# A fused recurrent scan: 32-column products, half-precision expert products in blocks of 8 steps, and another order on VectorE

## The reference, cut to what matters

```
# layer 1: a GRU cell over time, then a linear layer plus one of 8 rank-16 experts
gi = x @ W_ih + b_ih;  gh = h @ W_hh + b_hh
r = sigmoid(i_r + h_r);  z = sigmoid(i_z + h_z);  n = tanh(i_n + r * h_n)
h_new = (1.0 - z) * n + z * h
base_out = einsum('bsd,od->bso', x, W_base) + b_base
expert_idx = argmax(softmax(einsum('bsd,ed->bse', x, router_W)))
h = einsum('bsd,erd->bser', x, A) * onehot(expert_idx)[..., None]
out = base_out + einsum('bser,eor->bso', h, Bw) * 2
x = x + out
# layer 2: Runge-Kutta 4, four derivatives a step, x is the drive
i_couple = tanh(q) @ coupling.T
dq = q - q ** 3 / 3.0 - p + drive + i_couple + bias
dp = EPSILON * (q + ALPHA - BETA * p)
```

## Time and profile before

| | |
|---|---|
| median of the runs | 5070.73 us (5060.59 to 5075.04) |
| profiled execution | 5060.11 us, span 5058.5 us |
| TensorE busy | 4811.2 us (95%) |
| VectorE busy | 2748.1 us (54%) |
| ScalarE busy | 1687.5 us (33%) |
| GpSimd busy | 357.5 us (7%) |
| mean granted TensorE clock | 0.781 |

### The profile page before, as it was taken

The page is one execution under the profiler, slowest core; times in us unless marked ns, Lnnn a source line. Parts: engine busy times, 40 slices in busy tenths (PEclk is TensorE's granted clock), DMA queues, the critical chain, the costliest instruction groups (busy, mean ns, idle before and its releaser), DMA issues. The chain is left out here.

```text
span 5058.5 us, 197415 instructions
## 1 busy us (share of the span) xinstructions
PE 4811.2 (95%) x83680; PEld 3821.2 (76%) x83680; DVE 2748.1 (54%) x15134; ACT 1687.5 (33%) x7030; POOL 357.5 (7%) x1123
## 2 busy tenths in 40 slices
PE   8999989699999999999998699999999999999999
PEld 3335654699999999999997588789999999444444
DVE  3110020488888888888888726575553342344421
ACT  1101111245555555555554322233322221233320
POOL 1100010011111111111111100000000000000000
PEclk7999989555555555555555599999989999899999
DMA  3202330000000000000001000023320000100000
GB/s 106 106 10 111 150 124 8 16 4 5 5 5 5 5 5 5 5 5 5 5 5 53 13 9 2 33 71 94 92 77 3 3 3 2 47 8 8 10 7 33
DMA packets 52292, 159.62 MB, mean 32 GB/s; under 512 B 13873, under 2 KB 14001, under 8 KB 46272
## 3 DMA queue, kind: packets, MB, share of 16 engines
q1 hardware_dynamic: 45408, 130.70, 7.7%
q0 software_dynamic: 3712, 12.29, 0.7%
q10 hardware_dynamic: 2304, 4.20, 0.2%
HBM read 129.63 MB, written 17.17 MB: 29 GB/s over the span
## 5 line engine op out<-in xcount | busy, mean ns | idle before, releaser
L631 PE MATMUL k_ps<-k_hx,k_wlo 128*128 128x8 f16 x16384 | 604.9, 169 | 95.5 <-ACT k_hx L723 95.0
L631 PEld LDWEIGHTS k_ps<-k_hx,k_wlo 128*128 128x128 f16 x16384 | 545.7, 105 | 135.2 <-ACT k_hx L723 111.0
L634 PE MATMUL k_ps<-k_hl,k_whi 128*128 128x16 f16 x16384 | 590.0, 174 | 2.9 <-issue 0.4
L634 PEld LDWEIGHTS k_ps<-k_hl,k_whi 128*128 128x128 f16 x16384 | 519.4, 104 | 7.4 <-issue 1.8
L631 PE MATMUL g_ps<-g_hx,g_wlo 128*128 128x8 f16 x12288 | 434.2, 168 | 47.1 <-DVE g_hx L802 41.9
L634 PE MATMUL g_ps<-g_hl,g_whi 128*128 128x16 f16 x12288 | 436.9, 174 | 4.2 <-issue 4.1
L631 PEld LDWEIGHTS g_ps<-g_hx,g_wlo 128*128 128x128 f16 x12288 | 384.9, 104 | 59.0 <-DVE g_hx L802 52.3
L634 PEld LDWEIGHTS g_ps<-g_hl,g_whi 128*128 128x128 f16 x12288 | 385.1, 104 | 4.4 <-issue 4.4
L723 ACT ACTIVATE k_hx<-k_q 128x32 f16<-128x32 f32 x768 | 176.1, 229 | 567.1 <-DVE k_q L863 564.1
L1475 DVE TENSOR_REDUCE t_NM<-t_ps 128x1 f32<-128x512 f32 x256 | 165.0, 686 | 218.3 <-PE t_ps L1341 218.3
L863 DVE TENSOR_REDUCE k_q<-k_ps 128x32 f32<-128x96 f32 x768 | 196.8, 256 | 147.6 <-PE k_ps L634 122.0
(11 more groups left out here) (340 smaller groups left out, 8994.4 us busy)
## 6 DMA issues: line engine op xcount, KB each, us to landing
GRZ<-expert_places SPq DMA_DIRECT2D x64, 512.0 KB, 4.9
wm<-in_w_dram SPq DMA_DIRECT2D x4, 2816.0 KB, 10.2
GRZ<-in_w_dram SPq DMA_DIRECT2D x4, 2816.0 KB, 9.8
m_w<-in_w2a_dram SPq DMA_DIRECT2D x8, 1280.0 KB, 12.6
GRZ<-in_ue_dram SPq DMA_DIRECT2D x8, 1024.0 KB, 7.9
GRZ<-in_x_nat_dram SPq DMA_DIRECT2D x4, 1024.0 KB, 10.3
XT<-in_xT_dram SPq DMA_DIRECT2D x1, 4096.0 KB, 26.9
expert_rows<-wm SPq DMA_DIRECT2D x1, 4096.0 KB, 17.3
```

Source lines behind the costliest of these rows:

```text
L631: T.matmul(P[:,1,j*NB:(j+1)*NB],lo[:,kc,(m0+j)*128:(m0+j+1)*128],x[:,kc,:],start=(j==0 and kc==0),stop=False,skip_group_check=True)
L634: i=T.matmul(P[:,:,j*NB:(j+1)*NB],hi[:,kc,(m0+j)*128:(m0+j+1)*128],x[:,kc,:,:],start=False,stop=kc==KC-1,skip_group_check=True)
```

## The change

Five things are done together; what is computed stays the same.

1. Each gate and evaluation product streams 32 columns: the 8-column vector is read four times over (a broadcast view), the 16-column pair twice, and the copies land in unused columns of the same PSUM bank. The number of products and of weight loads stays.
2. Layer 1's base matrix, router and first factor are also split into two half-precision parts (by GpSimd, four passes over 2592 columns at the start of the scan). Each full-precision call becomes three half-precision ones (high weights by both state parts, low weights by the state). The states are now stored as half-precision parts for a whole block (`HX`, `HL`), and the full-precision state as two rows (`HF`).
3. Blocks of TL = 8 steps (64 columns) and LEAD = 17 rather than 16 and 29. Of every 8 iterations seven hold expert work: i = 0 and 1 six router products and three base products each, i = 2 and 4 fifteen base products each, i = 3 twelve and a transpose, i = 5 and 6 two full-precision calls each of the second factor.
4. The block's result is no longer added by VectorE (L826, which waited for TensorE), but copied out of PSUM by ScalarE (`expert_out`) and added by GpSimd (`results`); the bias is added once, by GpSimd, at the start.
5. VectorE's order: the limit of q (`limit`) is taken out of `end`; the z gate's `pre` comes first in an iteration, `low_part(t,0)` ahead of G0 and Q, `diff` leaves the place ahead of evaluation 3's `end` for evaluation 0, Q1 goes from evaluation 0 to 1, `state_full` behind evaluation 0's `end`, `low(s)` behind `low_part(t,1)`, and `low_part(t,2)` ahead of `pre(s,R_)`.

```diff
-LEAD, TL = 29, 16
+LEAD, TL = 17, 8
...
-        hx=sb('g_hx',[128,KC,NB],F16); hl=sb('g_hl',[128,KC,2,NB],F16); HS=sb('g_HS',[128,2,KC,TL,NB])
+        hx0=sb('g_hx0',[128,KC,NB],F16); hl0=sb('g_hl0',[128,2,KC,NB],F16); HF=sb('g_HF',[128,2,32]); HX=sb('g_HX',[128,2,KC,TL,NB],F16); HL=sb('g_HL',[128,2,2,KC,TL,NB],F16)
...
-                    T.matmul(P[:,1,j*NB:(j+1)*NB],lo[:,kc,(m0+j)*128:(m0+j+1)*128],x[:,kc,:],start=(j==0 and kc==0),stop=False,skip_group_check=True)
+                    T.matmul(P(j),lo[:,kc,(m0+j)*128:(m0+j+1)*128],bc(x[:,kc,:].unsqueeze(1),[128,4,NB]),start=(j==0 and kc==0),stop=False,skip_group_check=True)
-                    i=T.matmul(P[:,:,j*NB:(j+1)*NB],hi[:,kc,(m0+j)*128:(m0+j+1)*128],x[:,kc,:,:],start=False,stop=kc==KC-1,skip_group_check=True)
+                    i=T.matmul(P(j),hi[:,kc,(m0+j)*128:(m0+j+1)*128],bc(x(kc).unsqueeze(1),[128,2,2,NB]),start=False,stop=kc==KC-1,skip_group_check=True)
...
-                hs=HS[:,j%2].rearrange('p d t b -> p d (t b)')
+                hx=HX[:,j%2].rearrange('p d t b -> p d (t b)'); hS=HL[:,j%2,0].rearrange('p d t b -> p d (t b)'); lS=HL[:,j%2,1].rearrange('p d t b -> p d (t b)')
+                def base(u0,u1):
+                    for u in range(u0,u1):
+                        dc,d=u//4,u%4
+                        P=pso[:,dc*TN:(dc+1)*TN]; wh=wbh[:,d,dc*128:(dc+1)*128]; wl=wbl[:,d,dc*128:(dc+1)*128]
+                        T.matmul(P,wh,hS[:,d,:],start=u==0,stop=False,skip_group_check=True)
+                        T.matmul(P,wh,lS[:,d,:],start=False,stop=False,skip_group_check=True)
+                        T.matmul(P,wl,hx[:,d,:],start=False,stop=False,skip_group_check=True)
                 if i<2:
                     if i==0:
-                        e.wait_ge(g_h,TL*(j+1))
-                        if j==0: e.wait_ge(s_lw,64)
+                        e.wait_ge(g_lo,TL*(j+1)+1)
+                        if j==0: e.wait_ge(s_sp,4)
+                        e.wait_ge(l_e,j)
                     for d in (2*i,2*i+1):
-                        x=T.matmul(psh[:,0:136],hs[:,d,:],ar[:,d,:],start=d==0,stop=d==3)
+                        T.matmul(psh[0:TN,0:136],hS[:,d,:],arh[:,d,:],start=d==0,stop=False)
+                        T.matmul(psh[0:TN,0:136],lS[:,d,:],arh[:,d,:],start=False,stop=False)
+                        x=T.matmul(psh[0:TN,0:136],hx[:,d,:],arl[:,d,:],start=False,stop=d==3)
                     if i==1: x.then_inc(l_h,1)
-                if i==2: e.wait_ge(l_x,4*j)
-                if 2<=i<10:
-                    for u in (2*(i-2),2*(i-2)+1):
-                        dc,d=u//4,u%4
-                        T.matmul(pso[:,dc*128:(dc+1)*128],wb[:,d,dc*128:(dc+1)*128],hs[:,d,:],start=u==0,stop=False,skip_group_check=True)
-                if i==4:
+                    base(i,i+1)
+                if i==2: base(2,7)
+                if i==3:
+                    base(7,11)
                     e.wait_ge(l_ht,j+1)
-                    T.transpose(pst[:,0:128],ht[:],K.ident[:]).then_inc(l_tr,1)
-                if i in (10,11):
+                    T.transpose(pst[:,0:TN],ht[:],K.ident[0:TN,0:TN]).then_inc(l_tr,1)
+                if i==4: base(11,16)
+                if i in (5,6):
                     e.wait_ge(l_hm,j+1)
-                    for dc in (2*(i-10),2*(i-10)+1):
-                        x=T.matmul(pso[:,dc*128:(dc+1)*128],bw[:,dc*128:(dc+1)*128],hm[:],start=False,stop=True,skip_group_check=True)
-                    if i==11: x.then_inc(l_o,1)
+                    for dc in (2*(i-5),2*(i-5)+1):
+                        x=T.matmul(pso[:,dc*TN:(dc+1)*TN],bw[:,dc*128:(dc+1)*128],hm[:],start=False,stop=True,skip_group_check=True)
+                    if i==6: x.then_inc(l_o,1)
...
+            def expert_out(s):
+                j,i=s//TL-1,s%TL
+                if i!=7 or j<0 or j>=NT//TL: return
+                e.wait_ge(l_o,j+1)
+                if j>0: e.wait_ge(l_x,j)
+                A.activation(ex[:].rearrange('p d t b -> p (d t b)'),pso[:,0:KC*TN],ACT.Copy,scale=US).then_inc(l_e,1)
...
+            def results(s):
+                j,i=s//TL-1,s%TL
+                if i!=7 or j<0 or j>=NT//TL: return
+                e.wait_ge(l_e,j+1)
+                x=XT[:,:,:,j*TL:(j+1)*TL].rearrange('p d b t -> p d t b')
+                G.tensor_tensor(x,ex[:],x,ALU.add).then_inc(l_x,1)
+            e.wait_ge(s_lw,64)
+            both=wm[:,0:2592]; high,low_=split[:,0:2592],split[:,2592:5184]
+            G.tensor_scalar(both,both,SW,None,ALU.mult).then_inc(s_sp,1)
+            e.wait_ge(s_sp,1)
+            G.tensor_copy(high,both).then_inc(s_sp,1)
+            e.wait_ge(s_sp,2)
+            G.tensor_tensor(both,both,high,ALU.subtract).then_inc(s_sp,1)
+            e.wait_ge(s_sp,3)
+            G.tensor_scalar(low_,both,S,None,ALU.mult).then_inc(s_sp,1)
+            for dc in range(KC): G.tensor_scalar(XT[:,dc],XT[:,dc],bb[:,dc:dc+1],None,ALU.add).then_inc(s_bx,1)
...
-                elif i==12:
-                  e.wait_ge(l_o,j+1)
-                  for dc in (2*part,2*part+1):
-                    x=XT[:,dc,:,j*TL:(j+1)*TL].rearrange('p b t -> p t b')
-                    V.scalar_tensor_tensor(x,pso[:,dc*128:(dc+1)*128].rearrange('p (t b) -> p t b',b=NB),bb[:,dc:dc+1],x,ALU.add,ALU.add).then_inc(l_x,1)
...
-                e.wait_ge(k_q,t*4+k+2)
-                if k==3:
-                    e.wait_ge(k_out,t)
-                    V.tensor_scalar(q[:,0,:],qn[:],20.0/uq[0],-20.0/uq[0],ALU.min,ALU.max).then_inc(k_q0,1)
+                if k<3: e.wait_ge(k_q,t*4+k+2)
+            def limit(t):
+                e.wait_ge(k_q,t*4+5)
+                e.wait_ge(k_out,t)
+                V.tensor_scalar(q[:,0,:],qn[:],20.0/uq[0],-20.0/uq[0],ALU.min,ALU.max).then_inc(k_q0,1)
             for t in range(NT):
                 s=t+LEAD
+                if t>0:
+                    pre(s-1,Z_)
+                    limit(t-1)
+                    arg(s-1,Z_)
+                low_part(t,0)
+                if t>0: diff(s-1)
                 e.wait_ge(k_q0,t+1)
                 n_G=ch.did(stt(G0[:],p[:],-BETA*6/h,q[:,0,:]))
                 e.wait_ge(k_u,t+1)
                 n_Q=ch.did(stt(Q[:,0,:],q[:,0,:],1/3,E0[:]))
-                if t>0: pre(s-1,Z_)
-                low_part(t,0)
-                if t>0: arg(s-1,Z_)
+                if t>0: upd(s-1)
                 cubic(t,0)
-                ch.after(max(n_G,n_Q))
-                n_Q1=ch.did(stt(Q[:,1,:],G0[:],-a*EPS*h/6,Q[:,0,:]))
+                if t>0: state_half(s-1)
                 total(t,0,Q[:,0,:],n_Q)
-                if t>0: upd(s-1); state_half(s-1); state_full(s-1)
                 end(t,0)
 
+                if t>0: state_full(s-1)
                 e.wait_ge(k_aq,t*2+2)
                 n_B=ch.did(stt(B0[:,0,:],G0[:],-a*EPS*(1-kap)*h/6,AQ[:,0,:]))
                 n_C=ch.did(stt(B0[:,1,:],G0[:],cD,AQ[:,1,:]))
+                low_part(t,1)
+                n_Q1=ch.did(stt(Q[:,1,:],G0[:],-a*EPS*h/6,Q[:,0,:]))
                 low(s)
-                low_part(t,1)
                 ch.after(n_B)
                 n_K=ch.did(V.tensor_tensor(K2[:],Q[:,0,:],B0[:,0,:],ALU.add))
                 ch.after(n_C)
...
                 ch.after(max(n_W,n_X))
                 n_X=ch.did(stt(X[:,1,:],q[:,1,:],3*(1/3+e2*kap),X[:,0,:]))
                 n_W=ch.did(stt(W[:,1,:],q[:,1,:],a*hh*(2-2*kap+2*kap*kap),W[:,0,:]))
+                low_part(t,2)
                 pre(s,R_)
-                low_part(t,2)
                 arg(s,R_)
                 cubic(t,2)
                 ch.after(max(n_W,n_X))
...
                 ch.after(n_p)
                 V.tensor_scalar(p[:],pn[:],(20.0-SHIFT)/US,(-20.0-SHIFT)/US,ALU.min,ALU.max).then_inc(k_p,1)
                 total(t,3,X[:,3,:],n_X)
-                diff(s)
                 end(t,3)
+            limit(NT-1)
```

59 lines of the change are left out of this document (34 added, 25 removed).

## The result

The changed kernel takes 4980.18 us (median of 4 runs, 4976.26 to 5004.06) against 5065.66 (4 runs, 5055.51 to 5075.04) beside it: ratio 0.9845, 95% interval 0.9822 to 0.9868. It is faster by 1.55%. Forecast were 4820 us and a range from 4770 to 4965, so the direction was right and the gain a third of what was forecast; the time lies above the range. The profiled execution took 4976.7 us, with a span of 4975.1 against 5058.5.

The account below looks back on a forecast made before the run. The prediction took a chain of dependent steps to bound the scan's iteration, 7.36 us falling to 6.52. Lead -52, main part -113, tail -85 and GpSimd's split +3 sum to -247: 4813, median 4820 us, range 4770 to 4965.

Parts of the forecast that it names:

- VectorE's lists: Main part: VectorE's instruction order bounds the four evaluations at about 1.66, 1.64, 1.54 and 1.53 us, in all 6.37.
- The clock: Scan's main part: 32 columns a product raise TensorE's clock from 0.50 to 0.9 or more, and cost nothing at 0.50.
- The spacing: Time between TensorE's scan products at 2.4 GHz: between 13.4 ns (half) and 27 ns (unchanged).
- the rival that it stays near 27: Main part: the clock rises but product spacing stays near 27 ns; iteration 6.75 us, kernel 4875 us; chance 0.15.
- My rule of 0.23: VectorE's order: an instruction that needs its predecessor follows it after 0.23 us.
- TensorE looks full, but that is no bound: its iteration is a chain: Scan's main part: TensorE, busy 485 of 500 us, does not bound the iteration; a chain of dependent steps does.
- Experts: Main part: expert work adds 0.50 us an iteration at the low clock; halved at 2.4 GHz, it fits into a gap.
- The new order at the low clock: Main part at the low clock: VectorE's new order cuts the four evaluations from 7.03 to 6.58 us, 0.45 less.
- GpSimd's split: Lead: GpSimd's four passes take 26 us, wanted only 35 us in; cost taken as 3 us, ends 0 and 15.
- GpSimd has room for `results`: Main part: GpSimd, busy 68 of 500 us, has room to add the experts' results.
- Lead and tail: Scan's start and end: 12 lead iterations less give -52 us; the tail falls from 195.5 to 111 us, -85.
- The low clock as the reason to miss: Main part: the rival that the clock stays low; iteration 7.10 us, kernel 4960 us; chance 0.15.

Follow-up runs that it names:

- e1: The changed kernel with 8 and 16 columns a product again instead of 32: 5050.01 us, ratio 0.9977 against the kernel before.
- e3: The kernel before with only the 32 columns a product (part 1): 4995.84 us, ratio 0.9882 against the kernel before.
- e5: The changed kernel with a third VectorE order, in which `total` stands 0.1 to 0.3 us earlier: 4962.03 us, ratio 0.9808 against the kernel before.
- e10: The changed kernel with earlier `total`, results' add on VectorE, split and bias off GpSimd, and no expert work after the first block: 4868.37 us, one run.
- e2: The changed kernel with VectorE's old order in the scan (part 5 undone): 4977.96 us, ratio 0.9845 against the kernel before.
- e4: The kernel before with only the new VectorE order (part 5): 5066.61 us, ratio 1.0005 against the kernel before.
- e7: The changed kernel with the expert weights' split on ScalarE and VectorE and the bias added by ScalarE, not GpSimd: 4955.75 us, ratio 0.9786 against before.
- e6: The changed kernel with the experts' results added into XT by VectorE instead of GpSimd: 4973.73 us, ratio 0.9827 against the kernel before.

## Why the prediction was right and wrong, point by point

Two steps of the prediction failed in the main part: VectorE's lists, which are the larger part of what is missing in the kernel as it stands (0.41 of 0.57 us an iteration), and the supply of TensorE's instructions, which the forecast put at nothing and which would have kept the forecast out of reach with better lists too.

- **The clock** (right). 32 columns a product raise it to 0.97, and at half clock they cost nothing (tail: 6.73 us an iteration against 6.74). The change's gain is mainly this: 69 us by e1, 73 by e3.
- **The spacing** (wrong, but not decisive). I took something between 13.4 and 27 ns and gave 0.15 to the rival that it stays near 27. It is 25 ns: this rival's mechanism was what happened. The Trainium skill (TensorE: Matmul & The Clock Gate, section on 56 against 53.3 ns) has the right figure, 25 for 32 columns at the high level. The rival's price, 4875 us, was still too low by 105. At this spacing the products alone hold a clean evaluation at 1.61 (e5, e10), so that the 1.54 and 1.53 of evaluations 2 and 3 could not be had by any list.
- **VectorE's lists** (wrong size). I forecast 1.66, 1.64, 1.54 and 1.53. Measured are 1.79, 1.72, 1.65 and 1.61. The step that failed is the next `end` 0.22 us behind `total`: it is 0.30, four times an iteration, which is 0.32 of the 0.41 us that the lists lack. My rule of 0.23 came from instructions that write SBUF, while `total` writes PSUM and a reduction reads it; which of the two makes the difference no run separates. `low_part` stands at +0.75 in evaluation 0, not +0.67, since `pre` starts at +0.40. The expert work and the held-up instruction raise the median iteration, averaged over the eight kinds of step, by another 0.18 to 6.96 (0.05 forecast), and single longer iterations by 0.13 to 7.09 (0.10 taken, for the low level).
- **"TensorE looks full, but that is no bound: its iteration is a chain"** (true of the kernel before, wrong of the kernel after). This step would have decided with better lists too. I looked at TensorE's spacing and its columns, and not at the supply of its instructions. Before, 256 instructions took 4.1 us and needed 3.8; at 6.42 us an iteration they would have had to arrive in 3.5. At the rates seen, 3.76 to 3.82 us a block, 469.4 instructions need 6.9 to 7.0 us. So, as an estimate, 239 x 0.38 = 91 to 239 x 0.48 = 115 of the 136 us were out of reach, whatever VectorE's order. In the change itself the stops are 0.13 us an iteration. The limit shows when the lists get shorter: from after to e5 the typical iteration gains 0.19 and the mean 0.09, while the stops grow by 0.11. It does not explain e2, where the typical iteration is the same as in the change.
- **Experts** (right in size at the low clock, wrong at the high one). At the low clock they were to add 0.52 to a clean iteration; in e1 they add 0.52 to the typical one (6.83 to 7.35). The 7.10 forecast for the low clock missed e1's 7.38 by the lists, 6.83 against 6.58. At the high clock 0.05 were forecast and 0.18 came: 0.08 from VectorE's own expert work in evaluation 2, 0.08 from GpSimd's add, 0.02 from the expert products. Against the old form nothing is gained: e1 and e4, both at the low clock, are both at 7.38, since what evaluations 0 and 2 gain by the new form (0.08) GpSimd's add takes back. The blocks of 8 raise TensorE's instructions from 458.1 to 469.4 an iteration, which at 3.82 us for 256 is 0.17 us; e3 (7.040) and the change (7.086) have the same typical iteration, 6.97 and 6.96, and differ by their stops, 0.06 and 0.13. What the blocks of 8 bring is the shorter lead and tail.
- **The new order at the low clock** (wrong). 0.45 us were forecast for a clean iteration; e4 gains 0.19 there, and nothing in the mean (-0.02), because steps with base products lose 0.03.
- **GpSimd's split** (wrong size). I took 3 us, ends 0 and 15. By e7 the passes cost 23 us. I had asked when TensorE needs their results and not what VectorE does beside them. "GpSimd has room for `results`" failed for the same reason: 0.66 us in each block, 20 us in all by the intervals, though e6, which moved the add to VectorE, won too little to tell from nothing.
- **Lead and tail** (right). 12 lead iterations less are -52: with e7's lead the stretch is 51.1 us shorter than before. The tail is 114.5 us against 111.
- **The low clock as the reason to miss** (a rival at 0.15, 4960 us) gave nearly the right time with the wrong mechanism; e1, the change at the low clock, takes 5050.

The range of 4770 to 4965 held none of these costs together, since each case had the same lists and the same free lead.
